# Gated slot attention with two ternary FFNs: tap columns read in place, three of four key chunks transposed, the outputs' diagonal spread by GpSimd, the first state copied by ScalarE

## The reference

```python
q, k, v, w = (short_conv(h @ W, c) for ...)      # 4 taps per channel, then silu
w = l2norm(w); g = log_sigmoid(h @ Wf1 @ Wf2); beta = sigmoid(h @ Wb)
def step(Sk, Sv, q_t, k_t, v_t, w_t, g_t, b_t):
    gt = exp(g_t); bw = b_t * w_t
    Sk = Sk * gt + outer(k_t, bw)
    Sv = Sv * gt + outer(bw, v_t)
    a = softmax(q_t @ Sk * SCALE)
    return a @ Sv
gate = h @ Wg1 @ Wg2 + bg2
o = o * rsqrt(mean(o * o) + EPS) * norm_w * sigmoid(gate)
return o @ Wo
```

## Time and profile before

| what | value |
|---|---|
| median of 3 runs | 2888.96 us (2887.87 to 2891.6) |
| span of the profiled execution | 2888.6 us |
| mean granted TensorE clock | 0.989 |
| busy PE / DVE / ACT / POOL | 2796.3 / 2294.6 / 1626.3 / 1363.4 us |
| attention, first to last output | about 300 to 2622 us |
| an ordinary turn | 34.39 us, about 55 of 64 |

### The profile page before, as it was taken

One profiled execution on the slowest core, in us unless ns is written; L12 is line 12 of the kernel. 1 busy time (PEld: TensorE's weight loads), 2 busy tenths in 40 slices (PEclk: granted clock), 3 DMA queues, 4 the chain that ended last, 5 costly groups with the idle time before them and its releaser, 6 DMA issues. The chain is left out here.

```text
span 2888.6 us, 43596 instructions
## 1 busy us (share of the span) xinstructions
PE 2796.3 (97%) x13894; PEld 1952.6 (68%) x13894; DVE 2294.6 (79%) x5940; ACT 1626.3 (56%) x3682; POOL 1363.4 (47%) x2058
## 2 busy tenths in 40 slices
PE   6999899999999999999999999999999999989998
PEld 4888466666666666666666666666666666666887
DVE  7554488989986999988969998888799888984543
ACT  3101476766666776666667666666666667750010
POOL 0000466565654666566546566556456655660000
PEclk8999999999999999999999999999999999999999
DMA  4300311111111121111111211111111111105000
GB/s 171 143 15 15 109 37 37 34 48 35 48 33 58 48 66 34 49 34 49 33 58 48 67 34 48 37 48 30 58 58 57 34 52 36 52 22 193 15 15 30
DMA packets 90835, 151.06 MB, mean 52 GB/s; under 512 B 9200, under 2 KB 30832, under 8 KB 90096
## 3 DMA queue, kind: packets, MB, share of 16 engines
q1 hardware_dynamic: 90608, 148.29, 16.2%
HBM read 127.02 MB, written 21.23 MB: 51 GB/s over the span
## 5 line engine op out<-in xcount | busy, mean ns | idle before, releaser
L750 POOL TENSOR_TENSOR s<-s,tmp 128x256 f32<-128x256 f32 (+1 forms) x448 | 365.0, 815 | 307.3 <-DVE tmp L1043 289.5
L750 POOL TENSOR_TENSOR Y<-aT,D 128x256 f32<-128x256 f32 x384 | 282.2, 756 | 454.0 <-ACT aT L961 454.0
L1425 PEld LDWEIGHTS ps<-Y,S 128*128 128x128 f32 x1536 | 222.2, 192 | 162.8 <-issue 119.3
L750 POOL TENSOR_TENSOR X<-S,D 128x256 f32<-128x256 f32 x384 | 275.9, 718 | 119.0 <-ACT S L912 89.6
L223 ACT ACTIVATE sig<-up_ps 128x512 f32<-128x512 f32 x88 | 52.7, 599 | 451.5 <-PE up_ps L373 451.5
L373 PE MATMUL up_ps<-h_hi,wq 128*128 128x512 f32 x704 | 284.9, 405 | 11.6 <-DVE wq L284 9.7
L373 PE MATMUL up_ps<-h_lo,wq 128*128 128x512 f32 x704 | 280.9, 399 | 0.0
L1413 PEld LDWEIGHTS ps<-AM,XT 128*128 128x128 f32 x1536 | 215.8, 191 | 90.4 <-issue 71.7
L1381 PE MATMUL ps<-hT,slot_w 128*128 128x512 f32 x512 | 261.2, 593 | 5.3 <-DVE tmp L1043 5.3
L1381 PE MATMUL ps<-hT,slot_v 128*128 128x512 f32 x512 | 264.5, 599 | 0.6 <-DVE acc_w L1086 0.6
L1381 PE MATMUL ps<-hT,slot_k 128*128 128x512 f32 x512 | 262.1, 598 | 1.3 <-ACT beta L884 1.3
(11 more groups left out here) (194 smaller groups left out, 6943.0 us busy)
## 6 DMA issues: line engine op xcount, KB each, us to landing
slot_k<-in_wk_dram SPq DMA_DIRECT2D x64, 256.0 KB, 2.6
slot_w<-in_ww_dram SPq DMA_DIRECT2D x64, 256.0 KB, 2.6
slot_q<-in_wq_dram SPq DMA_DIRECT2D x64, 256.0 KB, 2.7
slot_v<-in_wv_dram SPq DMA_DIRECT2D x64, 256.0 KB, 2.7
wo<-in_wo_dram SPq DMA_DIRECT2D x60, 256.0 KB, 3.5
wq_dram<-wq SPq DMA_DIRECT2D x3, 2816.0 KB, 23.5
raw<-in_w_dram SPq DMA_DIRECT2D x8, 704.0 KB, 11.1
x_sb<-in_x_dram SPq DMA_DIRECT2D x4, 1024.0 KB, 6.7
```

The source lines that it names most:

```text
L750: return nc.gpsimd.tensor_tensor(out, in0, in1, op)
L1425: last = nc.tensor.matmul(pair_columns(bank[f"a2_{l}"], i), ck_(S[l], i), odd_targets(aT, i) if l == 1 else pair_columns(Y[l], i), start=T ...
```

## The change

Four edits, all in the attention phase:

1. `tap` and its copy are gone. ScalarE and VectorE read the columns from `per_head[:, head, column]`. The first unit waits once for the small inputs to be loaded.
2. `transpose("kT", ...)` and the scaling into `kv` cover three chunks, not four.
3. a2d moves from VectorE to GpSimd. It waits there for dg3 and stands ahead of the wait for aT and Y2. VectorE's first merge waits for GpSimd's a2d.
4. St0 moves from VectorE to ScalarE, after the copy s0 at the end of the turn. PE's k projection and VectorE's St1 wait for ScalarE's St0.

```diff
-DVE_LATE = ("... dg0 dg1 dg2 dg3 rs a2d a2_1 a2_2 ..."
+DVE_LATE = ("... dg0 dg1 dg2 dg3 rs a2_1 a2_2 ..."
-POOL_LATE = "ad8 ad16 ad32 adst ad64 y2 y4 y8 r1 y16 y32 y64 yst r2 r3 r4 r5".split()
+POOL_LATE = "ad8 ad16 ad32 adst ad64 a2d y2 y4 y8 r1 y16 y32 y64 yst r2 r3 r4 r5".split()
...
                 if late:
+                    pool.wait_ge(dve_late, after(DVE_LATE, "dg3", u))
+                    tt(chunks(A2), ident[:, :].rearrange("p (o n) -> p o n", o=1).to_broadcast([P, C, P]),
+                       dg[:, :].rearrange("p (c o) -> p c o", o=1).to_broadcast([P, C, P])).then_inc(pool_late, 1)
                     pool.wait_ge(act_late, after(ACT_LATE, "aT", u))
                     decay_rows(2, pool_late)
...
                     nc.scalar.activation(acc[x][:, :], bank[x][:, :], ACT.Copy,
-                                         scale=tap[:, at:at + 1]).then_inc(act_early, 1)
+                                         scale=per_head[:, n % NH, at:at + 1]).then_inc(act_early, 1)
...
                     nc.scalar.activation(level_one(s), level_one(bank["s0"]), ACT.Copy).then_inc(act_early, 1)
+                    act.wait_ge(pe_early, after(PE_EARLY, "U0", n))
+                    nc.scalar.activation(state[:, BLOCK[1] - 1, :], bank["U0"][:, 0:2 * P],
+                                         ACT.Copy).then_inc(act_early, 1)
...
-                    dve.wait_ge(act_late, after(ACT_LATE, "sg", u))
-                    nc.vector.tensor_scalar(tap[:, :], per_head[:, n % NH, :], 1.0, None,
-                                            ALU.mult).then_inc(dve_early, 1)
...
-                    dve.wait_ge(dve_late, after(DVE_LATE, "dg3", u))
-                    tt(chunks(A2), eye, own_rows(dg)).then_inc(dve_late, 1)
...
-                    dve.wait_ge(dve_late, after(DVE_LATE, "a2d", u))
+                    dve.wait_ge(pool_late, after(POOL_LATE, "a2d", u))
                     merge(1)
...
-                    tt(kv[:, :, 0:P], chunks(bank["kT"]), by_step).then_inc(dve_early, 1)
+                    tt(kv[:, 0:C - 1, 0:P], chunks(bank["kT"])[:, 0:C - 1, :],
+                       by_step[:, 0:C - 1, :]).then_inc(dve_early, 1)
...
-                    dve.wait_ge(pe_early, after(PE_EARLY, "U0", n))
-                    nc.vector.tensor_copy(state[:, BLOCK[1] - 1, :], bank["U0"][:, 0:2 * P]).then_inc(dve_early, 1)
                     dve.wait_ge(pe_early, after(PE_EARLY, "U1", n))
-                    dve.wait_ge(dve_early, after(DVE_EARLY, "St0", n))
+                    dve.wait_ge(act_early, after(ACT_EARLY, "St0", n))
...
-                    pe.wait_ge(dve_early, after(DVE_EARLY, "St0", u))
+                    pe.wait_ge(act_early, after(ACT_EARLY, "St0", u))
                     project("k", 0)
...
-                    transpose("kT", lambda c: ck_(k, c), pe_early)
+                    transpose("kT", lambda c: ck_(k, c), pe_early, C - 1)
```

More of the change, by code:

```diff
@@ L581, in attention_phase @@
         og = sb("og", [P, 2 * C, T])
-        tap = sb("tap", [P, 3 * KW + 1])
         TAP = {"q": 0, "k": KW, "v": 2 * KW, "w": 2 * KW}
@@ L935, in turn @@
                     nc.scalar.activation(sg[:, :], bank["gate"][:, :], ACT.Sigmoid,
-                                         bias=tap[:, BIAS:BIAS + 1]).then_inc(act_late, 1)
+                                         bias=per_head[:, u % NH, BIAS:BIAS + 1]).then_inc(act_late, 1)
                 if edge is not None:
@@ L942, in turn @@
                     act.wait_ge(pe_early, after(PE_EARLY, "k", n))
-                    act.wait_ge(dve_early, after(DVE_EARLY, "tap", n))
+                    if n == 0:
+                        act.wait_ge(small_full, 16 * SMALL)
                     first_tap("k")
@@ L1075, in turn @@
                 stats = n // NH + 1 if n % NH == NH - 1 and n // NH + 1 < NB else NB if n == UNITS else None
-                eye = ident[:, :].rearrange("p (o n) -> p o n", o=1).to_broadcast([P, C, P])
                 def own_rows(t):
```

15 lines of the change are left out of this document (8 added, 7 removed).

## The result

| | before | after |
|---|---|---|
| median | 2889.76 us (18 runs, 2886.51 to 2891.97) | 2881.22 us (18 runs, 2879.38 to 2891.38 and one of 7031.49) |
| profiled execution: span, mean clock | 2888.6 us, 0.989 | 2877.7 us, 0.992 |
| ordinary turn | 34.39 us | 34.28 us |

The ratio is 0.9975, with a 95% interval of 0.9968 to 0.9982: 7.2 us less (5.2 to 9.2), by the medians 8.5 us less. The forecast was 8.2 us less, 2880.8 us. One run of after took 7031.49 us, in the slow state; the ratio leaves it out, and without it the median is 2881.13 us.

The account below looks back on a forecast made before the run. PE's own work was taken to bound ordinary turns (34.39 us). Savings of 6.5 + 0.5 + 1.2 = 8.2 us from 2888.96 gave 2880.8 us, chance 0.66, range 2876.5 to 2888 us.

Parts of the forecast that it names:

- Three transposes: PE's transposes of k: one fewer saves 0.11 us in each of 59 turns, 6.5 us, bounds 0 and 7.0.
- oss earlier: Shorter kv scaling makes VectorE's oss earlier, shortening three PE waits for GpSimd's last X block: 0.5 us, bounds 0 and 1.0.
- Spread 1.3 us: Diagonal spread on GpSimd takes 1.3 us, first Y starts 0.6 us late, costing nothing in the 59 turns.
- a cover of 1.45 us for the forecast 1.5: GpSimd's spread may last about 1.5 us before PE waits; each further 0.1 us costs 5.9 us.
- Turns before an edge: Three turns: PE's waits for the merge and m64 shorten by 0.4 us together, 1.2 us in all, bounds 0.3 and 2.1.
- The term for m64: PE's 1.76 us wait before an edge loses the tap copy ahead of it: 0.1 to 0.18 us a turn.
- rivals A and B: Spread outlasts its cover, PE waits for Y4 each ordinary turn: A, 2889 us, chance 0.10; B, 2901 us, 0.08.
- VectorE operations on D that grow longer: Sign of a wrong forecast: these lengthen because GpSimd runs beside other ones, with w or a2_4 late for PE.
- Last turn: VectorE's gain meets a GpSimd Y chain that PE already waits for: 0, bounds -0.6 and +1.0 us.
- Turns two to five: GpSimd's chain to ScalarE's v gets about 0.3 us longer, As and oss come earlier: 0, bounds -1.0 and +1.2 us.
- Rival C, the clock: Shorter PE waits may spare two stretches at granted clock 0.50: 3.4 us more gained, 2877 us; chance 0.11.
- First state and taps at 0: State copy on ScalarE has 0.8 us or more of cover before the k projection; taps in place change no durations: 0.

Follow-up runs that it names:

- the kernel with 512 more columns: Changed kernel plus a second GpSimd spread of all 512 columns into a spare tile, behind the first: 2907.43 us.
- the one with the rows apart: Changed kernel with the next batch's statistics and normalisation rows moved from the turn before an edge into nine earlier turns: 2861.05 us, ratio to before 0.9903.

## Why the prediction was right, and where it was not

The total was right, 8.2 us forecast and 8.5 measured by the medians (7.2 by the ratio), and so was the largest term, with the mechanism behind it. That the sum of the others fits is luck. Smaller terms were wrong and cancelled: in the traces the turns at the edges cost 4.6 us more where 1.9 less were forecast (0.7 of it the transposes' share), and the part behind the last mark gave 4.8 and the stretch up to the end of the first five turns 3.0 where nothing was forecast.

- **Three transposes, 6.5 us: right.** The turn is 34.28 us. Alone they make 5.7 us by the medians.
- **oss earlier, 0.5 us: the size was off.** Stray waits were 2.1 us in all, more than the upper bound of 1.0, since besides the three waits for X their delay shows in other turns. They went in the single edits too, where kv kept its four blocks, so the shorter kv is not needed for it; they did not go in the kernel before with a second spread on GpSimd (1.5 us left). What they hang on stays open.
- **Spread 1.3 us: 1.05.** The estimate by the slope of Y, Yst and r was too long; the row of 384 columns taken without growth (1.0) would have been closer. The first Y was 0.31 us late, not 0.6. By the factor of two of the Trainium skill (GPSIMD Engine Reference, section Engine selection), 1.38 us, the estimate would have been worse: the trace has 1.046 against 0.692, a factor of 1.5. Cost 0 in ordinary turns, and a cover of 1.45 us for the forecast 1.5: right.
- **Turns before an edge, 1.2 us less: wrong sign in its larger part.** The term for m64 (1.76 to 1.60 us) was right. The step that failed is "without the spread, the w taps start ... 0.3 us earlier", so the merge comes 0.3 us earlier. VectorE did start 0.32 us earlier, and GpSimd's products came 0.23 us later, so the four rows of the normalisation met four GpSimd products: 3.91 us instead of 2.73, and the wait grew by 0.84 us. (With the spread alone three of the four were slow, and the wait grew by 0.16 to 0.19.) The prediction had read the price in the earlier trace rows, where GpSimd's products took 1.02 us instead of 0.73, and used it only for GpSimd's own length, in rivals A and B. It did not ask what VectorE pays when the other engine comes first. In its last paragraph it names VectorE operations on D that grow longer as a sign; they did, from 417 to 944 ns, and cost nothing there, as VectorE's slack in an ordinary turn took them.
- **Last turn, 0, bounds -0.6 and +1.0: the size was off.** The part behind the last mark lost 4.8 us. PE's waits for Y and the merge went from 3.3 to 2.1 us there, and the trace has 6.8 us less at a granted 0.50, worth up to 3.4. The gain is not the spread's: with the spread undone, and with the three transposes alone, this part is as short (315.3 us); with the spread alone it is 2.7 us less than in before.
- **Turns two to five, 0, bounds -1.0 and +1.2:** the first five turns took 1.7 us less, and the part ahead of the first mark, which has no term, 1.3 less. Among the single edits these two columns move by as much without a pattern (169.6 to 171.2 and 332.5 to 334.3 us), so this is not shown to be the change's.
- **Rival C, the clock:** the opposite happened at the edges (five low stretches instead of three), and behind the last mark there was less (6.8 us instead of 13.7, up to 2640 us). The five stretches that the prediction counts are not all alike: the last, at 2600.8 us, is 6.8 us long.
- **First state and taps at 0:** their steps are right (1.2 us of cover, taps at the same durations, turns unchanged), yet each alone makes about 3 us by the medians. About 2 of them are the stray waits, by one trace of each kernel; the rest stays open.

## What to carry to other kernels

Before moving an operation between VectorE and GpSimd, list for each turn what runs beside what afterwards, not only who waits for whom: here moving one instruction shifted the two engines against each other by 0.55 us before an edge, instructions of VectorE took about twice as long, and only the turns without slack paid for it. The parts of a small change need not add when the kernel has waits that small shifts remove, so test each part and the whole. And when one turn in sixteen is the late one, spread its extra work over the turns that have idle time: that was worth more than twice the change itself.

## What was unexpected of the hardware

- Two engines that collide do not share the loss evenly. VectorE's spread of 512 columns kept 0.69 us, GpSimd's of the same size beside it went from 1.04 to 1.54 us; D<-u_g of VectorE went from 0.42 to 0.94 us while the GpSimd product beside it kept 0.73. In a near tie the records' start does not tell who pays: the normalisation's second row, 0.09 us ahead of the Y in nine turns, kept 0.54 us in five and took 1.10 in four.
- A PE that the records show as busy without a pause can wait: 0.53 us in each turn under 34.81 us of "busy" in 34.83. The check is the spacing from start to start. So the sentence ahead of the prediction that a stretch in which PE is always busy has no pause in it does not hold. The prediction's reading of the earlier trace rows, that a turn full of PE has no wait in it, is right by the spacing of the matmuls in that turn (0.11 us from one to the next for 128 columns, 0.22 for 256 and 0.43 for 512, without exception), but the row did not prove it.
- In the kernel with 512 more columns, with 0.55 us more of such short waits in each turn and a merge wait of 1.86 us, the attention part from 345 to 2600 us had no stretch at the lower clock; the changed kernel had five at the edges alone, and the one with the rows apart, without those waits, still three. What decides it was not tested.
